# A seven-product query-key multiplication in a fused attention and feed-forward kernel

## What is computed

```
q, k, v = split(xn @ qkv_w + qkv_b)          # 16 heads of 16 channels
q, k    = q / |q|, k / |k|                   # norm over each head's 16 channels
att     = (q @ (k.T @ v)) @ proj_w + proj_b  # no softmax: k.T @ v is 16 x 16 a head
ffn     = relu(xn @ W1 + b1) @ W2 + b2       # 1024 hidden units
```

## Time and profile before

| | us |
|---|---|
| median of three runs | 554.02 |
| profiled execution, span from its first to its last instruction | 552.4 |
| TensorE busy (2590 matmuls) | 547.7 |
| VectorE busy | 398.5 |
| ScalarE busy | 286.9 |
| GpSimd busy | 119.4 |

### The profile page before, as it was taken

The page is one execution under the profiler, slowest core; times in us unless marked ns, Lnnn a source line. Parts: engine busy times, 40 slices in busy tenths (PEclk is TensorE's granted clock), DMA queues, the critical chain, the costliest instruction groups (busy, mean ns, idle before and its releaser), DMA issues.

```text
span 552.4 us, 8714 instructions
## 1 busy us (share of the span) xinstructions
PE 547.7 (99%) x2590; PEld 460.2 (83%) x2590; DVE 398.5 (72%) x791; ACT 286.9 (52%) x529; POOL 119.4 (22%) x150
## 2 busy tenths in 40 slices
PE   9999999999999999999999999999999999999997
PEld 7888888888888888888888888888888888888896
DVE  6977788567795876858667587775777767684655
ACT  4785654556336563465644556455553655533421
POOL 4242424202052020420213202331024201050100
PEclk9999999999999999999999999999999999999999
DMA  8522134343413434134341343315333251314312
GB/s 259 167 87 50 33 83 93 83 105 83 107 20 86 98 85 95 24 86 98 85 88 31 93 92 84 81 38 113 71 90 67 45 107 38 79 37 93 96 39 76
DMA packets 141413, 45.34 MB, mean 82 GB/s; under 512 B 133330, under 2 KB 136402, under 8 KB 141396
## 3 DMA queue, kind: packets, MB, share of 16 engines
q1 hardware_dynamic: 139280, 44.61, 34.7%
q10 hardware_dynamic: 2116, 0.53, 0.5%
HBM read 20.98 MB, written 8.39 MB: 53 GB/s over the span
## 4 chain that ended last, share of the span: by engine, by line
PE 99%; DVE 0%; issue 0%
PE o_bank L1169 12%; PE o_bank L1170 12%; PE o_bank L1171 12%; PE w_bank L1169 11%; PE w_bank L1170 11%; PE w_bank L1171 11%; PE v_bank L1169 7%; PE v_bank L1170 7%; PE v_bank L1171 7%; PE kv_bank L1307 3%; PE g_bank L1307 3%; PE kv_bank L1312 1%; PE g_bank L1312 1%; PE kv_bank L1323 1%; PE w_bank L1361 1%; PE g_bank L1171 0%
## 5 line engine op out<-in xcount | busy, mean ns | idle before, releaser
L957 DVE SCALAR_TENSOR_TENSOR h_lo<-w_bank,h_hi 128x512 fp32r<-128x512 f32 x128 | 87.4, 683 | 38.2 <-ACT h_hi L607 36.5
L607 ACT ACTIVATE h_hi<-w_bank 128x512 fp32r<-128x512 f32 x128 | 76.4, 597 | 66.5 <-PE w_bank L1171 66.4
L1169 PE MATMUL w_bank<-xT_hi,w_hi 128*128 128x512 f32 x254 | 99.9, 393 | 0.0
L1170 PE MATMUL w_bank<-xT_lo,w_hi 128*128 128x512 f32 x254 | 99.2, 391 | 0.0
L1171 PE MATMUL w_bank<-xT_hi,w_lo 128*128 128x512 f32 x254 | 98.9, 389 | 0.0
L1169 PE MATMUL o_bank<-h_hi,w_hi 128*128 128x512 f32 x240 | 93.5, 389 | 0.0
L1170 PE MATMUL o_bank<-h_lo,w_hi 128*128 128x512 f32 x240 | 93.4, 389 | 0.0
L1171 PE MATMUL o_bank<-h_hi,w_lo 128*128 128x512 f32 x240 | 93.4, 389 | 0.0
L405 POOL TENSOR_TENSOR xn_lo<-xn,xn_hi 128x256 fp32r<-128x256 f32 x56 | 42.5, 759 | 217.6 <-ACT xn_hi L517 213.4
L420 POOL TENSOR_TENSOR y_sb<-y_sb,y_rows 128x256 f32<-128x256 f32 x56 | 52.5, 941 | 123.7 <-DVE y_rows L1001 103.2
L585 ACT ACTIVATE qk_sq<-v_bank 128x512 f32<-128x512 f32 x64 | 38.3, 598 | 72.2 <-PE v_bank L1171 72.2
(11 more groups left out here) (213 smaller groups left out, 921.4 us busy)
## 6 DMA issues: line engine op xcount, KB each, us to landing
y_rows<-blocks SPq DMA_DIRECT2D x256, 32.0 KB, 1.9
x_sb<-x SPq DMA_DIRECT2D x15, 512.0 KB, 3.5
y_sb<-x SPq DMA_DIRECT2D x60, 128.0 KB, 3.3
out<-y_sb SPq DMA_DIRECT2D x58, 128.0 KB, 2.5
xT_raw<-blocks SPq DMA_DIRECT2D x224, 32.0 KB, 1.9
y_sb<-w SPq DMA_DIRECT2D x4, 256.0 KB, 5.1
x_sb<-x SPq DMA_DIRECT2D x2, 256.0 KB, 3.0
w_raw<-w SPq DMA_DIRECT2D x2, 256.0 KB, 7.4
```

The costliest lines, as they stand in the source:

```text
L607: nc.scalar.activation(h_hi[:, j % RING, :], w_bank[j % 2][:], ACT.Relu).then_inc(h_done, 1)
L957: nc.vector.scalar_tensor_tensor(h_lo[:, r, :], w_bank[j % 2][:], 0.0, h_hi[:, r, :].bitcast(F32), ALU.max, ALU.subtract).then_inc(h_lo_do ...
L1169: nc.tensor.matmul(to, left[0], right[0], start=first, stop=False, skip_group_check=shared)
L1170: nc.tensor.matmul(to, left[0], right[1], start=False, stop=False, skip_group_check=shared)
```

## The change

For halves 3 to 15 the 2 x 2 block product of a pair of tiles n and n + 2 (two tiles of 128 tokens, two chunks of 128 input channels, q and k columns of 256) is made by Strassen's scheme in Winograd's form: seven block products of three matmuls with 256 columns, instead of eight. Tile n has the blocks x00 and x01, tile n + 2 the blocks x10 and x11. What goes into the products besides the plain blocks are four sums of x blocks (the "forms") and four of weight blocks. GpSimd makes the x forms once a half (`x_forms`, when the moved x has landed) and the weight forms once (`weight_forms`); ScalarE and VectorE split the x forms (`x_forms_high`, `x_forms_low`). Partial results are passed between four half banks: ScalarE copies two of them (`qk_seed`), VectorE adds twice (`qk_seed`, `qk_sum`). The lists of all engines are written out for each kind of half, with new places for several older steps too. The core of the diff, GpSimd first:

```diff
+            def x_forms(s):
+                wait(pool, x_moved, 16 * MOVES * (s - 1))
+                first, second = slice(0, PAIR * P), slice(PAIR * P, HALF)
+                nc.gpsimd.tensor_tensor(xf_raw[:, 0:2], xT_raw[:, :, second],
+                                        xT_raw[:, 0].rearrange("p (a n) -> p a n", a=PAIRS),
+                                        ALU.subtract).then_inc(xf_sums_done, 1)
...
+                nc.gpsimd.tensor_tensor(xf_raw[:, X11_X01_X00], xT_raw[:, 1, second], xf_raw[:, X01_X00],
+                                        ALU.subtract).then_inc(xf_sums_done, 1)
...
+                nc.gpsimd.tensor_tensor(xf_raw[:, X10_X11_X01_X00], xT_raw[:, 1, first], xf_raw[:, X11_X01_X00],
+                                        ALU.subtract).then_inc(xf_raw_done, 1)
...
+            def even_half(b, s):
+                split_xn(s + 2, 0)
+                x_forms(s + 2)
```

The new steps of ScalarE, and the first and last steps of its even half:

```diff
+            def x_forms_high(s):
+                wait(act, xf_raw_done, s - FORMS_FROM + 1)
+                copy(xf_hi[:].rearrange("p f (b n) -> p f b n", b=PAIR),
+                     xf_raw.rearrange("p f (n b) -> p f b n", b=PAIR)).then_inc(xf_hi_done, 1)
+
+            def qk_seed(s, n):
+
+                wait(act, qk_begun, pairs_done(s, n))
+                wait(act, qk_copied, TILES * s + 2 * n)
+                copy(qk_21, qk_11)
+                wait(act, qk_22_summed, pairs_done(s, n) - 1)
+                copy(qk_fifth[:], qk_22).then_inc(qk_seeded, 1)
...
+                h_high(s, 2)
+                k_high(s, 0)
+                x_forms_high(s + 1)
+                qk_seed(s + 1, 0)
+                h_high(s, 3)
...
+                qk_pair_out(s + 1, 1, 1, 1)
+                h_high(s + 1, 1)
+                qk_root(s + 1)
+                yT_out(b, 0, 0)
+                yT_out(b, 0, 1)
+                xT_high(s + 2, 0)
```

The new steps of VectorE, its even half, and the first steps of its odd half:

```diff
+            def x_forms_low(s):
+                wait(dve, xf_hi_done, s - FORMS_FROM + 1)
...
+            def qk_seed(s, n):
+
+                wait(dve, qk_21_sixth_in, pairs_done(s, n))
+                nc.vector.tensor_tensor(qk_12, qk_21, qk_fifth[:], ALU.add).then_inc(qk_12_seeded, 1)
+
+            def qk_sum(s, n):
+
+                wait(dve, qk_21_seventh_in, pairs_done(s, n))
+                nc.vector.tensor_tensor(qk_22, qk_21, qk_fifth[:], ALU.add).then_inc(qk_22_summed, 1)
...
+            def even_half(b, s):
+                xT_low(s + 1, 1)
+                divide(0, 0, q_done)
+                h_low(s, 2)
+                x_forms_low(s + 1)
+                transpose_q(s, 0)
+                k_low(s, 0)
+                variance(s + 2, b + 1, 0)
+                h_low(s, 3)
+                h_low(s, 4)
+                spread(s + 2)
+                qk_seed(s + 1, 0)
+                qk_sum(s + 1, 0)
+                transpose_x(s + 2)
+                h_low(s, 5)
...
+                sum_pair_squares(s + 1, 1, 1)
+                bound(s + 1)
+                h_low(s + 1, 1)
+                norms(s + 1)
+                divide(1, 1, k_done)
...
+            def odd_half(b, s):
+                divide(0, 1, q_done)
+                h_low(s, 2)
+                xT_low(s + 1, 0)
+                x_forms_low(s + 1)
+                k_low(s, 1)
+                h_low(s, 3)
+                transpose_q(s, 1)
```

TensorE's even half. `qk_begin` and `qk_second` and `qk_third` are two block products each (6 matmuls of 256 columns), `qk_fourth` is one:

```diff
+            def even_half(b, s):
+                ffn_up(s, 0, 2)
+                ffn_down(s, b, 0, 0)
+                ffn_up(s, 0, 3)
+                ffn_down(s, b, 0, 1)
+                ffn_up(s, 0, 4)
+                ffn_down(s, b, 0, 2)
+                qk_begin(s + 1, 1, 0, b)
+                gather(s, b, 0)
+                qk_second(s + 1, 1, 0)
+                ffn_up(s, 0, 5)
+                qk_third(s + 1, 0)
+                ffn_down(s, b, 0, 3)
+                ffn_up(s, 0, 6)
+                qk_fourth(s + 1, 1, 0)
+                ffn_down(s, b, 0, 4)
+                qk_begin(s + 1, 1, 1, b)
+                ffn_up(s, 0, 7)
+                ffn_down(s, b, 0, 5)
+                qk_second(s + 1, 1, 1)
+                ffn_up(s + 1, 1, 0)
+                qk_third(s + 1, 1)
+                ffn_down(s, b, 0, 6)
+                ffn_up(s + 1, 1, 1)
+                qk_fourth(s + 1, 1, 1)
+                ffn_down(s, b, 0, 7)
```

581 lines of the change are left out of this document (439 added, 142 removed).

## The result

The changed kernel takes 574.8 us (median of four runs, 574.4 to 575.2) against 553.9 us (median of four as well), a ratio of 1.037 (95% interval 1.036 to 1.039). It is slower, by 20.9 us where the forecast had 5.5; the range of 549 to 572 does not hold it. The profiled execution spans 573.3 us instead of 552.4, the same 20.9 us.

The account below looks back on a forecast made before the run. TensorE was taken as the bound (busy 547.7 of 552.4 us); -5.7 + 6.3 + 0.2 + 4.2 + 0.5 = +5.5 us gave a span of 557.9 and a predicted 559.5 us, 8-in-10 range 549 to 572.

Parts of the forecast that it names:

- turns between GpSimd and VectorE: At the half starts: two-input SBUF operations of both engines take turns, each waiting until the other's operation is over.
- rival 3: Delay feeds itself: forms meet norms before `end`, VectorE free at 3.2, holds 2.9 and 1.4 us; 574 us, chance 0.14.
- matmul gain, 13 halves: Query-key product, halves 3 to 15: 42 short matmuls replace 24 long ones, 0.44 us each half, 5.7 us saved.
- even-half holds, 6: Start of the even half: late `h_low(2)` and `k_low` hold TensorE 1.05 us, six times, 6.3 us.
- odd-half holds, 6: Start of the odd half: forms delay norms and divides, `ffn_up(4)` held 0.7 us, six times, 4.2 us.
- last batch and ends: 0.2 us for the last batch's even half, 0.5 us for the last odd half and the turn from the first batch.
- weight forms (`project(0)`): Before the loop: 9 us of weight forms made once in GpSimd's idle time after 73 us, costed at nothing.
- 0.44 us is left: Matmul saving per half: 0.68 us at equal column cost, less 0.006 us for each of 42 short matmuls.
- VectorE being free at 1.66: Even half: VectorE free 1.66 us after TensorE's first matmul, fixed because it waits for the attention's last output.
- its walk: Odd-half start: norms at F + 2.5, `h_low` at F + 6.4 or up to 8.2 with turns; `ffn_up(4)` due F + 6.8.
- F: Time reference at the turn to the odd half: the start of the last `ffn_down` of the half on TensorE.
- 0 to 1.4: Range in us for the hold at the odd half's start; half of the upper end, 0.7 us, was taken.

Follow-up runs that it names:

- e3: Changed kernel with GpSimd's x forms, residual adds and weight-form sums cut to one column, the weight forms' copy and low part left whole: span 552.8 us.
- e5: Changed kernel, complete, with the sum and low part of the weight forms made in four operations of 256 columns each: span 571.1 us.
- e6: Kernel before, complete, with each 512-column query-key matmul issued as two of 256 columns: span 558.3 us.
- e14: Changed kernel, complete, with GpSimd's even-turn forms and adds later, quartered weight forms behind kv_low, odd-half second divide behind k_low, ends mended: 564.1 us, ratio 1.022.
- e1: Changed kernel with GpSimd's three x form operations per half cut to one column: span 560.0 us.
- e2: Changed kernel with GpSimd's eight residual additions in batches 0 to 6 cut to one column: span 563.2 us.
- e7: Kernel before, complete, plus GpSimd's three x form operations per half, written into a spare buffer that nothing reads: span 552.1 us.
- e15: Kernel of e14 with GpSimd's four adds of the even half's rows cut to one column and their wait for the second divide dropped: span 560.5 us.
- e4: Changed kernel, complete, with only VectorE's lists reordered: h_low(2) ahead of divide in both halves, k_low ahead of the transpose in the even half: span 575.3 us.
- e8: Changed kernel, complete, with GpSimd's adds of the odd half's rows moved behind the splitting of x in the next even half: span 571.3 us.
- e10: Changed kernel with GpSimd's x forms cut to one column only at the turn from even to odd half: span 568.9 us.
- e9: Changed kernel with GpSimd's x forms cut to one column only at the turn from odd to even half: span 567.3 us.
- e11: Changed kernel, complete, with GpSimd's x forms waiting for VectorE's norms (odd turn) or first divide (even turn): 573.5 us, ratio 1.041.

## Why the prediction was wrong

The direction, the places (`ffn_up(4)` behind `h_low(2)`, the gather behind `k_low`, xT_lo and divide stretched, norms under the forms) and the cause, turns between GpSimd and VectorE, are as it had them. What failed are terms of the sum: the matmul gain was taken more than three times too large, the weight forms and what follows a hold were taken at nothing, and the even half was sized on a start of VectorE that did not stay where it was. The time was that of rival 3, and its mechanism only in part. Term by term, predicted and measured:

| term | predicted us | measured us | by |
|---|---|---|---|
| matmul gain, 13 halves | -5.7 | -1.7 | e3: 0.26 per batch |
| even-half holds, 6 | +6.3 | +8.2 | intervals |
| odd-half holds, 6 | +4.2 | +4.3 | intervals |
| last batch and ends | +0.7 | +2.4 | intervals |
| weight forms (`project(0)`) | 0 | +2.6 | intervals, e5 |
| lower clock behind two holds | 0 | +3.0 | intervals, windows |
| slow first interval behind each hold | 0 | some +2 | 0.11 x 18 |
| sum | +5.5 | +20.8 | span: +20.9 |

The terms add up, but they are not independent: as e5 shows, a stretch at the lower clock can take a later hold away.

**The matmul gain** failed first: 5.7 us predicted, 1.7 measured. "0.44 us is left" counts the pitch of the short matmuls alone, and e6 shows that pitch right; what was left out is that a long matmul behind a short one is slower too, 0.03 us each time. The row for it stood in the trace of before: the chunk that follows the gather at 299.84. With 17 returns in a batch against three before this takes 0.4 of the 0.87 us away.

**The weight forms**, "made once, in GpSimd's idle time after 73 us. I cost them at nothing". GpSimd was idle there and VectorE was not. The rule that the prediction itself used for the even half, that an operation with two operands waits for the whole of GpSimd's (2.41 against 2.37 us), was not applied to a 2.39 us operation next to `kv_low`, which `project(0)` waits for. Of the 2.6 us some 2.0 are theirs: 0.53 stays in e3, where their first operation is down to one column, and in e14, where they start behind `kv_low`, and belongs to the splitting of xn. With them came the first of the two stretches at 1.2 GHz; the prediction had no term for the clock.

**The even half** had its size from VectorE being free at 1.66, of which the prediction said that it "cannot move, since it waits for the attention's last output". It moved to 2.2, because the divide ahead of the spreads was held by the forms. Rival 3 named this way and put it at 3.2 us with holds of 2.9 and 1.4 us; they are 1.6 and 0.8. Its holds are nearly twice too large, its matmul gain is over three times too large, and it knew nothing of the weight forms and the clock; that the sum is 574 confirms none of it.

**The ends** were put at 0.2 us for the last even half and 0.5 for the rest, and are 1.8 and 0.7. In the last even half VectorE's xT_lo (2.22 us) and `k_low` (1.76) meet the adds, so that standing earlier in the list did not save them.

**The odd half** has its walk right in the steady batch: norms at F + 2.4, the forms at F + 1.7, three turns lost, and 0.82 us of hold where the middle of 0 to 1.4 was taken. That the six add up to 4.3 where 4.2 stood is partly luck: four of them are held at `ffn_up(4)` by 0.8 to 1.4 us, two not at all, and 0.55 us is a wait for ScalarE that was not foreseen.

That the holds come from turns is shown by e1, e2 and e3; that it takes the new order as well, by e7. The Trainium skill says the same (SBUF — State Buffer, Who interferes with whom): a VectorE operation with two SBUF inputs contends with a GpSimd operation that reads SBUF, and whichever issues first holds the other until it is done; the trace agrees, 2.45 us for `kv_low` beside 2.39 us. By the same section of the Trainium skill a tensor_scalar can contend as well; the 1.18 us of e15 and the 1.89 us of e3, instead of 0.23, agree.

What stays open: why the clock fell behind some holds and not behind others, and whether another order of all three lists could win the 0.26 us per batch that e3 shows to be there. No run leaves out the copy and the low part of the weight forms, so that the 1.34 us which e3 loses at 79.81 are put down to them by the timeline alone; e14, where they start behind `kv_low` and in quarters, has no such hold and begins the loop's first even half at 86.70.

## What to carry to other kernels

When a change puts an operation on GpSimd, do not price it by GpSimd's idle time. List what VectorE does with two SBUF operands in that stretch, and take for each the full length of the GpSimd operation that it can meet; if TensorE waits for one of them, cut the GpSimd operation small or move it. Then ask how late the list already is: the same three operations cost nothing in the old order (e7) and some 12 us in the new one (e1, without its clock). And a mend that only delays the lesser engine's work has to be followed down the queue behind it, here from the adds to the move of q, the move of x, and back to the forms; it is the distance to TensorE's steps that counts, and that shrinks when TensorE is held less.

## What the runs showed of the hardware

- A 512-column matmul stream that follows 256-column matmuls runs for one chunk at 0.23 to 0.24 us per matmul instead of 0.227: about 0.03 us a return (e6, eight returns, in every batch).
- The first interval of 512-column matmuls behind a hold at a chunk is 0.34 us instead of 0.227 (305.77 to 306.11, 331.93 to 332.27), and behind a hold at the gather 0.31 (309.61 to 309.92), so a hold costs 0.08 to 0.11 us more than its wait.
- A hold of 2.55 to 2.58 us at `project(0)` was followed by some 3.4 us at 1.2 GHz in the changed kernel, e2, e4, e8 and e10, and by none in e1, e9 and e11 with a hold of the same length. A hold of 1.94 us at 233.6 was followed by one in the changed kernel, and one of 1.98 us in the same place of e5 and one of 2.45 us there in e10 by none. The eight holds of 0.7 to 1.4 us in the changed kernel's loop never were.
- VectorE's TENSOR_SCALAR of 128x128, with one SBUF operand, waited for GpSimd (1.18 us in e15, 1.89 us in e3, instead of 0.23), and so did its copy of 128x256 into `kv_hi` (0.71 instead of 0.29 us, e3); its transposes and its operations with one of two operands in PSUM did not (1.25 us at 300.02 and 0.68 us at 305.04, both beside GpSimd's adds).
